# Cross-attention with quantised scores: GpSimd's layer norms subtract the mean instead of adding its negative

## The reference, cut to what matters

```python
def _layernorm(x, axis=-1, eps=1e-05):
    m = jnp.mean(x, axis=axis, keepdims=True)
    v = jnp.var(x, axis=axis, keepdims=True)
    return (x - m) / jnp.sqrt(v + eps)
...
x = x + _L1_attn_ref(_layernorm(x, axis=-1), ...)
x = x + _L1_xattn_ref(_layernorm(x, axis=-1), ctx_2048, ...)
x = x + _L1_ffn_ref(_layernorm(x, axis=-1), ...)
```

## Time and profile before

| | |
|---|---|
| median of 3 runs | 540.27 us |
| lowest, highest | 539.93, 540.74 us |
| profiled execution, own time | 537.92 us |
| its span, first to last instruction | 536.2 us |
| busy in the span | PE 434.5, DVE 412.1, ACT 341.9, POOL 253.0 us |
| mean granted TensorE clock | 0.966 |

### The profile page before, as it was taken

The page is one execution under the profiler, slowest core; times in us unless marked ns, Lnnn a source line. Parts: engine busy times, 40 slices in busy tenths (PEclk is TensorE's granted clock), DMA queues, the critical chain, the costliest instruction groups (busy, mean ns, idle before and its releaser), DMA issues. The chain is left out here.

```text
span 536.2 us, 11095 instructions
## 1 busy us (share of the span) xinstructions
PE 434.5 (81%) x3915; PEld 285.1 (53%) x3915; DVE 412.1 (77%) x825; ACT 341.9 (64%) x636; POOL 253.0 (47%) x456
## 2 busy tenths in 40 slices
PE   7988857767988888587788888887888779899885
PEld 3536734445555565334445555454446338788664
DVE  5899898849599776999999999999995854542244
ACT  2664237944578465399999999999994114445340
POOL 5756210006089465304454464645322048888870
PEclk9999886989899998899999999999999999999999
DMA  8850000000006300399999999999995978996548
GB/s 284 240 185 12 0 2 1 1 0 1 1 1 109 51 1 1 41 173 182 154 183 178 188 177 185 184 193 194 182 189 112 307 238 227 238 238 122 86 75 246
DMA packets 169862, 69.46 MB, mean 130 GB/s; under 512 B 142352, under 2 KB 167632, under 8 KB 169808
## 3 DMA queue, kind: packets, MB, share of 16 engines
q1 hardware_dynamic: 162288, 58.53, 53.6%
q0 software_dynamic: 4704, 7.61, 7.8%
q10 hardware_dynamic: 2816, 2.62, 1.6%
HBM read 27.56 MB, written 7.62 MB: 66 GB/s over the span
## 5 line engine op out<-in xcount | busy, mean ns | idle before, releaser
L939 ACT ACTIVATE A<-ps,b,sq 128x1024 int16<-128x1024 f32 x128 | 153.2, 1203 | 15.5 <-POOL b L653 7.4
L1855 DVE TENSOR_REDUCE nm<-ps 128x1 f32<-128x1024 f32 x128 | 152.1, 1213 | 10.1 <-PE ps L1294 8.8
L1294 PE MATMUL ps<-big,ctx_sb 128*128 128x512 bf16 x256 | 78.4, 388 | 30.1 <-ACT A L939 26.3
L653 POOL TENSOR_SCALAR b<-nm,sq 128x1 f32<-128x1 f32 x120 | 31.8, 265 | 98.7 <-DVE nm L1855 68.5
L1365 PEld LDWEIGHTS ps<-VI,A 128*128 128x128 f16 x1024 | 42.9, 96 | 20.7 <-issue 3.4
L1930 DVE TENSOR_TENSOR AT<-AT,ps 128x128 f32<-128x128 f32 x32 | 9.2, 287 | 50.3 <-ACT AT L961 50.3
L719 POOL DMA_INDIRECT A<-x_rows,slot_token x32 | 35.3, 1103 | 25.3 <-DMA x_rows<-ctx_sb 15.9
L1365 PE MATMUL ps<-VI,A 128*128 128x16 f16 x1024 | 44.3, 170 | 0.6 <-DMA A<-A 0.3
L1294 PEld LDWEIGHTS ps<-big,ctx_sb 128*128 128x128 bf16 x256 | 15.2, 97 | 52.0 <-ACT A L939 41.3
L731 POOL DMA_INDIRECT sums<-XN,slot_token x22 | 35.4, 1610 | 7.6 <-issue 4.6
L990 PE MATMUL ps<-identb 128*128 128x512 bf16 x135 | 36.1, 413 | 2.6 <-POOL identb L518 2.6
(11 more groups left out here) (315 smaller groups left out, 1026.3 us busy)
## 6 DMA issues: line engine op xcount, KB each, us to landing
A<-in SPq DMA_DIRECT2D x32, 256.0 KB, 3.7
A<-in SPq DMA_DIRECT2D x32, 128.0 KB, 4.3
A<-in SPq DMA_DIRECT2D x2, 1024.0 KB, 14.0
A<-A SPq DMA_TRANSPOSE x112, 3.5
X<-in SPq DMA_DIRECT2D x2, 512.0 KB, 4.5
big<-in SPq DMA_DIRECT2D x1, 1024.0 KB, 9.2
ctx_sb<-in SPq DMA_DIRECT2D x1, 1024.0 KB, 16.4
sums<-zeros SPq DMA_DIRECT2D x2, 512.0 KB, 4.8
```

What stands on the lines that cost most here:

```text
L653: g.tensor_scalar(b5[:, n % 4:n % 4 + 1], nm5[:, n % 4:n % 4 + 1], sq5[:, q, h:h + 1], LN255, ALU.mult, ALU.add).then_inc(S["pbias5_ready" ...
L939: a.activation(Y5[:, n % YB, :], ps[:, 2 * ((n + 1) % 3):2 * ((n + 1) % 3) + 2, :], ACT.Exp, scale=sq5[:, q, h:h + 1], bias=b5[:, n % 4:n ...
L1294: done = T.matmul(ps[:, 2 * ((n + 1) % 3) + c, :], QT5[:, q % 2, h // 2, h % 2, :], KT5[:, h // 2, c * 512:(c + 1) * 512], start=True, sto ...
L1855: v.tensor_reduce(nm5[:, n % 4:n % 4 + 1], ps[:, 2 * ((n + 1) % 3):2 * ((n + 1) % 3) + 2, :].rearrange("p a c -> p (a c)"), AX.X, ALU.max, ...
```

## The change

GpSimd's apply takes the mean from mv and subtracts it. The instruction that wrote nmean and its buffer are gone, and the counts of rstd_e follow.

```diff
-        nmean = sb("nmean", [P, NT])
...
                 g.tensor_scalar(veps[:, lo:hi], mv[:, lo:hi, 1], EPS, None, ALU.add).then_inc(S["rstd_e"], hi - lo)
-                done = 8 + NT + 2 * (first + hi - lo - 1)
-                if first < len(LN_ORDER):
-                    g.tensor_scalar(nmean[:, lo:hi], mv[:, lo:hi, 0], -1.0, 0.0, ALU.mult, ALU.add).then_inc(S["rstd_e"], hi - lo)
-                    pool.wait_ge(S["rstd_e"], done)
-                else:
-                    pool.wait_ge(S["rstd_e"], done - 1)
+                pool.wait_ge(S["rstd_e"], 8 + NT + first + hi - lo - 1)
                 g.tensor_tensor(rstd[:, lo:hi], veps[:, lo:hi], neghalf[:, 0:hi - lo], ALU.pow).then_inc(S["rstd_ready"], hi - lo)
...
-                g.tensor_scalar(XN[:, t, :], X[:, t, :], nmean[:, t:t + 1], rstd[:, t:t + 1], ALU.add, ALU.mult).then_inc(S["xn_ready"], 1)
+                g.tensor_scalar(XN[:, t, :], X[:, t, :], mv[:, t, 0:1], rstd[:, t:t + 1], ALU.subtract, ALU.mult).then_inc(S["xn_ready"], 1)
```

## The result

The changed kernel takes 542.77 us (median of 22 runs, 540.50 to 545.36), the kernel before 540.25 in the same comparison (22 runs, 537.94 to 543.18): ratio 1.005, interval 1.0035 to 1.0064. The forecast was 538.9 in 537.9 to 540.2; the result lies outside, on the slower side.

What follows compares the result with a forecast made beforehand. VectorE and ScalarE, coupled unit by unit, bound the loop, stalled by GpSimd work ahead of the bias; 1.9 us for nmean, 0 for the apply, less 0.5 given back, makes 1.4 faster: 540.27 to 538.9 us, range 537.9 to 540.2.

Steps and rivals of the forecast that it cites:

- The changed apply: GpSimd's apply of XN, subtracting the mean instead of adding its negative: 0 taken, bounds -0.3 to +0.3 us in all.
- The removed instruction: nmean on GpSimd, ahead of ScalarE's bias: 0.27 us per norm, on the path seven times, 1.9 us off.
- What the sooner loop runs into: SP's queue of DMA transposes in the exponential loop: takes back 0 to 0.9 us of the gain, 0.5 taken.
- give-back: Part of the loop's gain lost to waits for DMA transposes: 0 to 0.9 us, 0.5 taken.
- The transposes hold the loop: Rival: transpose reserve gone from the first saturated tile, only 0.55 us of gain survives, 539.7 us; chance 22%.
- The power starts no sooner: Rival: in GpSimd's norm, nmean may have covered veps's completion, so that wait replaces all 0.27 us, 540.3 us; chance 10%.
- Slower, by the subtract: Rival: GpSimd's apply takes longer with subtract, TensorE waiting behind; at 0.45 us more, 1.3 us slower, 541.5 us; chance 6%.
- The signs named: Trace signs for the forecast: fewer GpSimd instructions, shorter ScalarE idle, cadence near 22.56 us, more transpose waits, apply at 547 ns.

Runs made afterwards that it cites:

- e2: Changed kernel with the apply adding the mean from mv instead of subtracting it (XN shifted): 538.98 us, ratio 0.9991 to the kernel before.
- e1: Kernel before with nmean kept as plus the mean and the apply subtracting it: 545.83 us, ratio 1.0156 to the kernel before.
- e10: Kernel before with nmean alone moved ahead of its unit's bias, veps and the power behind it, a repeat measurement: 538.69 us, ratio 0.997.
- e5: Kernel before with veps and nmean moved ahead of their unit's bias, the power alone behind it: 537.40 us, ratio 0.9971.
- e9: Kernel before with a second fast add-form apply, read by nobody, ahead of the real one: 549.49 us, ratio 1.0148.
- e8: Kernel before, unedited, profiled once more: 540.75 us.
- e7: Changed kernel, unedited, profiled once more: 544.64 us.

## Why the prediction was wrong, point by point

**The step that failed** is "The changed apply": "I take 0, since the two differ only by a sign", with bounds of 0.04 us either way. It measured +0.69 us each, 0.57 of it on the path at seven places: 4.0 us, by which the forecast gain became a loss. The bounds came from a tensor_tensor subtract (668 ns) beside a multiply (630), another instruction; the step itself said that no row shows the form, and then took the nearest rows as if they held it. The range did not follow that warning: for a form that no row shows, two neighbours 38 ns apart are no bound.

**The removed instruction: right.** 0.27 us per norm, on the path seven times. e2 has it alone: 1.92 us forecast as 1.9, cadence 22.56 forecast as near 22.56. In the changed kernel it is seen before the slow apply has bitten: from the first exponential to n = 13 of the first tile it takes 17.90 us instead of 18.18. The halves add up per tile, -0.27 and +0.57 for the +0.29 measured, and over seven places, -1.9 and +4.0 for the +2.05 of the stretch. As whole stretches e1 and e2 do not (+5.9 - 1.9 = 4.0): e1's surplus is the lowered clock, which the changed kernel does not have in the loop.

**What the sooner loop runs into: too much by 0.5 us.** The give-back was 0 in e2, the lower of the two bounds. The reading that SP's queue issued without a hole, 23.01 us per tile, and "does not move once it is full", was wrong. In e10 it issued without a hole as well, and faster:

```profile
282.16 21.36 SPq L476 DMA_TRANSPOSE A<-A  x14
...
373.43 25.63 SPq L476 DMA_TRANSPOSE A<-A  x17
```

(373.43 - 282.16) / 4 = 22.82 us per tile, with a longest issue of 2.5 us instead of the 3.0 of the earlier trace rows. So an unbroken row of issues is not by itself the queue's pace. Nor is it free: the loop ran four tiles at 22.49, the queue fell behind by 0.3 us in each, and the reserve covered it at the price of 1.9 us of waits, no more than before. The bound exists, near 22.65 in e5, and it is not one number.

**The rivals.** *The transposes hold the loop*: not in the changed kernel, whose view of waits lists none for a transpose, and not in e2, which ran at 22.56 and kept the whole 1.9 us where this rival would have left 0.55. *The power starts no sooner*: refuted, 290.26 + 0.22 = 290.48 and the power at 290.57, 0.09 us, exactly the gap of L541 and L543; so a wait on veps covers nothing that nmean had hidden. *Slower, by the subtract*: this is what happened, with its place (the apply, TensorE directly behind), its point of decision (beyond 0.27 us more) and its sign. Its size fell short, 0.45 where 0.69 was measured. Its formula would with 0.69 give 7 x 0.42 = 2.9 us, against 2.05 in the loop, since 0.12 or so of each apply was absorbed. Its chance of 6% was low for a price that no row held.

**The signs named.** 14 instructions fewer: yes. Power 0.09 behind veps: yes. ScalarE's idle before those exponentials at 0.03 or less: 0.07 and 0.04 us at the first two, then 0.02 at the other five, and the idle for biases fell by 3.5 us. Cadence near 22.56: no, 23.12. More waits for transposes: no, none. Apply at 547 ns: no, 1234.

## What to carry to other kernels

An algebraic rewrite that swaps one operation of an instruction for its neighbour (add for subtract) is not free until a row shows that instruction with that operation on that engine; a neighbouring instruction's row is not a bound. Before deleting a small instruction by moving its work into a large one, compare what stands on the path: here 0.27 us were removed and 0.69 put in the same place. And look first whether the small instruction can run in a gap that is there anyway: moving nmean ahead of the bias it delayed gave at least what deleting it could. And a wait that grows on TensorE can cost more than its length, when the granted clock falls behind it: here 1.4 us a time.

## What the runs showed of the hardware

- **Subtract in GpSimd's tensor_scalar.** 1234 ns against 547 at 128 x 256 f32, 0.79 to 0.82 us against 0.44 at 128 x 128: about 2.7 ns more per column, in either place, with per-partition values; 0.80 us with constants, without a twin. GpSimd's tensor_tensor subtract is not slow in this way (668, with one bf16 operand, against 630 for a multiply). VectorE does the same form (X, mv, rstd, subtract and multiply) in this view by line and form of the changed kernel in 577 ns, near GpSimd's fast 547 and under half of its 1234; VectorE's add was not run beside it:

```profile
L1472 DVE TENSOR_SCALAR XN<-X,mv,rstd 128x256 f32<-128x256 f32 x32 | 16.5, 577 | 1.6 <-POOL rstd L542 1.6
```

- **TensorE's clock at the end of the loop.** It falls in the loop in e1 and e9, as shown there, and at the loop's end in others. In the profile of the changed kernel the eight matmuls of L1367 at 409.27 take 1.87 us; before, 1.03 us at 405.11. The granted clock there is 0.5, the lower level of 1.2 GHz, right after TensorE had waited 1.44 us for an exponential; before it is not lowered, after the same 1.44 us:

```profile
408.32 0.90 PE L1269 MATMUL ps<-identh,A 128*128 128x128 f16 x8 [1.44 <-ACT A L933]
...
409.27 1.87 PE L1367 MATMUL ps<-big,identb 128*128 128x256 bf16 x8
```

```profile
404.45 0.62 PE L1275 MATMUL ps<-identh,A 128*128 128x128 f16 x8 [1.44 <-ACT A L939]
...
405.11 1.03 PE L1373 MATMUL ps<-big,identb 128*128 128x256 bf16 x8
```

From that first row to the next transpose of XN TensorE takes 4.59 us (408.32 to 412.91) instead of 3.20 (404.45 to 407.65). It is not the change's: the kernel before has it too in its second profile (e8). How much of it reaches the end is not shown: what follows the last exponential took 132.2 us in the changed kernel and 134.3 in e7, both with the lowered clock, 131.4 before and 134.3 in e8, of which only the second has it. The spans of the two first profiles differ by 4.6 us (540.8 - 536.2): 1.8 ahead of the loop, which starts at 225.7 us before and 227.5 after though the code ahead of it is the same up to 197 us, 2.05 in it, and 0.7 behind it. Such differences come and go between executions of one kernel; over all profiles the first exponential started at 224.2 to 227.7 us and what follows the last one took 131.4 to 134.8. A profile of one execution is to be read by stages here, and the total by many runs.
